# Mamba stage: the next image in twelve pieces between C's spreads, and two lists of waits in another order

## What is computed

```python
def _mamba(x, W_in, conv_w, conv_b, W_x, W_dt, b_dt, A_log, D_skip, W_out):
    ...
    u = silu(causal_conv4(xi) + conv_b)
    x_dbl = u @ W_x.T
    dt = softplus(x_dbl[..., :dt_rank] @ W_dt.T + b_dt)
    Bs, Cs = ...                       # 16 states each, per pixel
    A = -exp(A_log)
    def step(h, inp):                  # along the 3136 pixels
        dA = exp(dt_t[..., None] * A)
        h = dA * h + (dt_t * u_t)[..., None] * B_t[:, None, :]
        return (h, einsum('bdn,bn->bd', h, C_t))
    ...
    return y * silu(z) @ W_out.T

x = x + _L0(_gn(x)); x = x + _L1(_gn(x)); x = x + _L2(_gn(x))
x = x + _L3(_gn(x))      # _L3: m(x1) + x1*s1 + m(x2) + x2*s2, layer norms, projection
```

## Time and profile before

| | us |
|---|---|
| time, median of 3 runs (lowest, highest) | 6452.99 (6450.01, 6456.59) |
| the profiled execution, its own time | 6451.64 |
| its span in the trace | 6449.8 |
| busy: PE / DVE / ACT / POOL | 4509.5 / 5081.2 / 2524.9 / 4686.1 |
| Mamba stage, from 3215 us | about half of the span |

### The profile page before, as it was taken

The page is one execution under the profiler, slowest core; times in us unless marked ns, Lnnn a source line. Parts: engine busy times, 40 slices in busy tenths (PEclk is TensorE's granted clock), DMA queues, the critical chain, the costliest instruction groups (busy, mean ns, idle before and its releaser), DMA issues. The chain is left out here.

```text
span 6449.8 us, 55394 instructions
## 1 busy us (share of the span) xinstructions
PE 4509.5 (70%) x15006; PEld 2441.9 (38%) x15006; DVE 5081.2 (79%) x4078; ACT 2524.9 (39%) x3885; POOL 4686.1 (73%) x3364
## 2 busy tenths in 40 slices
PE   4888656565564756553257888888788887887887
PEld 2666523332323333232123433433344343443433
DVE  4888726776766677666558989989899898998998
ACT  1112111111111111110056666666666666666664
POOL 1666617777777777777457878878788787887887
PEclk8777766566565665655589999999999999999999
DMA  5556723434435344343235444444444544444443
GB/s 156 116 120 128 146 73 104 123 115 143 122 104 153 104 122 121 119 124 105 87 113 150 151 144 149 152 144 150 143 155 142 153 151 146 149 138 154 154 152 117
DMA packets 377439, 853.16 MB, mean 132 GB/s; under 512 B 194828, under 2 KB 237732, under 8 KB 372784
## 3 DMA queue, kind: packets, MB, share of 16 engines
q1 hardware_dynamic: 292432, 618.03, 32.7%
q0 software_dynamic: 84672, 231.32, 11.9%
HBM read 766.91 MB, written 56.48 MB: 128 GB/s over the span
## 5 line engine op out<-in xcount | busy, mean ns | idle before, releaser
L2035 POOL TENSOR_TENSOR ma_hc<-ma_h,ma_cc 128x784 f32<-128x784 f32 x1024 | 1885.1, 1848 | 628.5 <-DVE ma_h L1937 496.4
L827 POOL DMA_INDIRECT fl_quad<-table,fl_idx x1764 | 1698.5, 963 | 694.4 <-issue 537.0
L1592 PE MATMUL ma_bank<-ma_hc,ident 128*128 128x392 f32 x4096 | 1529.9, 495 | 74.5 <-POOL ma_hc L2035 74.5
L1937 DVE TENSOR_TENSOR_SCAN ma_h<-ma_da,ma_state,ma_bank 128x784 f32<-128x784 f32 x768 | 1417.4, 1846 | 168.6 <-POOL ma_hc L2035 67.0
L1810 ACT ACTIVATE ma_da<-ma_dt,ma_a_neg 128x784 f32<-128x784 f32 x1024 | 948.1, 943 | 496.1 <-DVE ma_h L1937 479.3
L978 DVE TENSOR_TENSOR fl_part<-fl_quad,fl_bank 128x2304 f32<-128x2304 f32 x196 | 500.3, 2552 | 709.6 <-DMA fl_quad<-table,fl_idx 697.0
L1925 DVE TENSOR_TENSOR ma_bank<-ma_dtu,ma_bank 128x784 f32<-128x784 f32 x1024 | 980.7, 958 | 32.7 <-PE ma_bank L1579 32.2
L1592 PEld LDWEIGHTS ma_bank<-ma_hc,ident 128*128 128x128 f32 x4096 | 709.0, 190 | 504.1 <-POOL ma_hc L2035 79.0
L1119 PE MATMUL fl_bank<-ident,fl_tap 128*128 128x128 f32 (+1 forms) x980 | 242.8, 410 | 935.8 <-DVE xres L996 875.0
L1579 PE MATMUL ma_bank<-ma_bc,ma_sel 96*128 96x512 bf16 (+1 forms) x2048 | 517.0, 334 | 451.4 <-DVE ma_h L1937 439.9
L986 DVE TENSOR_REDUCE fl_tap<-fl_part 128x576 f32<-128x2304 f32 x196 | 796.6, 4064 | 0.1
(11 more groups left out here) (220 smaller groups left out, 6095.8 us busy)
## 6 DMA issues: line engine op xcount, KB each, us to landing
ma_cc<-c_rows SPq DMA_DIRECT2D x512, 784.0 KB, 4.2
mx_win<-flat SPq DMA_DIRECT2D x64, 878.0 KB, 10.2
fl_quad<-table,fl_idx POOLq DMA_INDIRECT x1764, 2.7
table<-fl_xt SPq DMA_DIRECT2D x64, 392.0 KB
mx_mask<-in_c_mask SPq DMA_DIRECT2D x56, 294.0 KB, 4.4
ma_xs<-ma_x SPq DMA_DIRECT2D x64, 196.8 KB, 5.2
ma_xs<-ma_x SPq DMA_DIRECT2D x64, 196.5 KB, 5.7
mx_xf<-flat SPq DMA_DIRECT2D x8, 816.0 KB, 15.5
```

Source lines behind the costliest of these rows:

```text
L827: gp.indirect_dma_start(quad[i][:, kk, :], None, table, bass.IndirectOffsetOnAxis(ap=idx[i][:, kk:kk + 1], axis=0))\
L1592: ins = pe.matmul(ps_y[:, t, :], ident[:], hc[:, n % RH, at], start=False, stop=(n == DS - 1))
L1937: dve.tensor_tensor_scan(h[:, i % RH, :], da[:, i % RH, :], ps_bu[i % 2], before, ALU.mult, ALU.add).then_inc(scand, 1)
L2035: gp.tensor_tensor(hc[:, i % RH, :], h[:, i % RH, :], cc[:, i % (NGRP * GRP), :], ALU.mult)\
```

## The change

**The image in pieces.** `image` is replaced by `piece(x, n)` for n = 0 to 11: pieces 0 to 7 are the eight transfers of the shuffled half as before (8 partitions each), pieces 8 to 11 are the ordered half in four transfers of 16 partitions. The same 1568 KB go to the same places; x_in now counts 12 x 16. In the period q = 1 the pieces stand one behind a spread each: pieces 0 to 2 behind the next group's spreads 1 to 3 in group 0 (the wait for `centred` stands ahead of piece 0), 3 to 6 behind spreads 4 to 7 of group 1, 7 to 10 behind the next group's spreads 0 to 3, and 11 behind those. The first image, ahead of the loop, is loaded by the same 12 transfers in a row.

**The order of waits.** In `times_b`, `scan` (DVE) and `times_c` (POOL) the same waits are written in another order: the semaphore of the work that ends last is named last. No instruction of arithmetic is changed, and PE's and ACT's instructions stand as before.

```diff
@@ -1298,7 +1298,7 @@
     AHEAD = 3
     NGRP, GRP = 4, 2
     BR = 2 * DS
-    XIN = 9 * 16
+    XIN = 12 * 16
     with ExitStack() as ctx:
         s = Space(nc, ctx, "ma")
         xa = s.sb("xa", [P, PIX])
@@ -1408,12 +1408,14 @@
             for half, name in ((lower, "m_s1"), (upper, "m_s2")):
                 sp.dma_start(vec[half, 7:8], k[name].partition_broadcast(CH)).then_inc(consts, 16)
 
-            def image(x):
-                sp.dma_start(xa[lower, :], x).then_inc(x_in, 16)
-
-                for j in range(8):
-                    sp.dma_start(xa[CH + 8 * j:CH + 8 * j + 8, :],
-                                 x.rearrange("(g j) n -> j g n", j=8)[j]).then_inc(x_in, 16)
+            def piece(x, n):
+
+                if n < 8:
+                    sp.dma_start(xa[CH + 8 * n:CH + 8 * n + 8, :],
+                                 x.rearrange("(g j) n -> j g n", j=8)[n]).then_inc(x_in, 16)
+                else:
+                    own = slice(16 * (n - 8), 16 * (n - 8) + 16)
+                    sp.dma_start(xa[own, :], x[own]).then_inc(x_in, 16)
 
             def halves(dram, b, q):
 
@@ -1461,26 +1463,37 @@
 
             def period(b, q, post=True, norm=True, prep=True):
                 Q = NQ * b + q
+                more = q == 1 and not (isinstance(b, int) and b == NB - 1)
+                if more:
+                    later = k["x3"][bass.ds(b + 1, 1)].rearrange("b c n -> (b c) n")
                 for g in range(2):
                     G = 2 * Q + g
                     for j in range(NGRP, DS // GRP):
                         spread_c(G, g, j)
                         if j == NGRP and g == 0 and post:
                             load_residual(b, q - 1)
-                        if j == NGRP + 1 and g == 0 and q == 1 and not (isinstance(b, int) and b == NB - 1):
-                            sp.wait_ge(centred, START + NQ * b + NQ)
-                            image(k["x3"][bass.ds(b + 1, 1)].rearrange("b c n -> (b c) n"))
+                        if g == 1 and more:
+                            piece(later, j - 1)
                     if g == 0 or prep:
                         put_c(G + 1, 1 - g)
                         for j in range(NGRP):
                             spread_c(G + 1, 1 - g, j)
+                            if g == 0 and j == 1 and more:
+                                sp.wait_ge(centred, START + NQ * b + NQ)
+                            if g == 0 and j >= 1 and more:
+                                piece(later, j - 1)
+                            if g == 1 and more:
+                                piece(later, NGRP + 3 + j)
+                        if g == 1 and more:
+                            piece(later, 11)
                     if g == 1:
                         if norm:
                             stack(b, q + 2)
                         if post:
                             store(b, q - 1)
 
-            image(k["x3"][0])
+            for n in range(12):
+                piece(k["x3"][0], n)
             stack(0, 0)
             stack(0, 1)
             put_c(0, 0)
@@ -1919,19 +1932,20 @@
 
             def times_b(G, g, i):
                 V = DS * G + i
-                dve.wait_ge(bready, START + V + 1)
                 if i == 0:
                     dve.wait_ge(dtud, START + G + 1)
+                dve.wait_ge(bready, START + V + 1)
                 dve.tensor_tensor(ps_bu[i % 2], dtu[g][:], ps_bu[i % 2], ALU.mult).then_inc(bud, 1)
 
             def scan(G, m, g, i):
 
                 V = DS * G + i
+                if not (isinstance(V, int) and V < RH):
+                    dve.wait_ge(saved, START + (DS // 2) * G + (i - RH) // 2 + 1)
+                    dve.wait_ge(hcd, START + V - RH + 1)
                 dve.wait_ge(expd, START + V + 1)
+
                 dve.wait_ge(bud, START + V + 1)
-                if not (isinstance(V, int) and V < RH):
-                    dve.wait_ge(hcd, START + V - RH + 1)
-                    dve.wait_ge(saved, START + (DS // 2) * G + (i - RH) // 2 + 1)
 
                 before = zcol[:] if m == 0 else state[:, g, i:i + 1]
                 dve.tensor_tensor_scan(h[:, i % RH, :], da[:, i % RH, :], ps_bu[i % 2], before,
@@ -2025,13 +2039,14 @@
             def times_c(G, i, after_low=None):
                 V = DS * G + i
                 j = i // GRP
-                gp.wait_ge(scand, START + V + 1)
                 if after_low is not None:
                     gp.wait_ge(lowd, START + after_low)
                 if i % GRP == 0:
                     gp.wait_ge(cin[j % NGRP], START + 32 * G + 16 * (j // NGRP) + 16)
                 if not (isinstance(V, int) and V < RH):
                     gp.wait_ge(yd, START + V - RH + 1)
+
+                gp.wait_ge(scand, START + V + 1)
                 gp.tensor_tensor(hc[:, i % RH, :], h[:, i % RH, :], cc[:, i % (NGRP * GRP), :], ALU.mult)\
                   .then_inc(hcd, 1)
 
```

## The result

| | before | after | forecast |
|---|---|---|---|
| median of the runs, us | 6452.05 (6450.01 to 6456.59) | 6364.4 (6361.5 to 6366.82) | 6306 (6298 to 6332) |
| profiled execution, us | 6451.64 | 6361.5, span 6359.6 | 6305.6 |
| ratio to before | 1 | 0.9863, interval 0.9846 to 0.988 | 0.977 |

The change is a gain of 88 us where 146 were forecast. The time is that of rival A, 6366, and the question is whether A's reason is right too. All the gain lies in the Mamba stage; I start where the prediction started.

What follows compares the result with a forecast made beforehand. DVE was taken to bound the Mamba stage. From the profiled 6451.64 us, 87 for the image and 59 for the order of waits gave 6305.6, so 6306 us for the median, range 6298 to 6332.

Steps and rivals of the forecast that it cites:

- rival A: DVE's order of waits brings nothing, since the number of instructions stays and sets the gaps: 6366 us, 7%.
- What bounds the kernel: Mamba stage: DVE is the bound, busy 90.59 of 95.34 us; a change is worth what it takes from DVE's gaps.
- Part one, the image: Seven loop periods with an image load fall to their neighbours' length once the block ahead of spread 6 goes: 87.0 us.
- The prices at the dear end: Pieces in the loop: 1.5 us delay per spread; 2 us more at the last piece would cost 14 us; 0 taken.
- On small transfers: Skill's fixed 2 us per transfer: three more per image cost 6 us, 42 in all if on the path, else nothing.
- 0, within half a us: First image, ahead of the loop: the same bytes in another cut change the time by 0, within half a us.
- Part two, the order of waits: DVE in the loop: the register instruction moves ahead of the wait for bud and is covered by the multiply: 59 us.
- the steps from multiply to scan are 1.04 or 1.05 throughout: Sign in DVE's timeline that the order of waits worked: the 1.13 us steps are gone.
- a bound from below: Order of waits priced by the written-out period without register instructions: 95.34 - 93.33 = 2.01 us, 56 us over 28 periods.
- the written-out period has the same PE work at the shorter step and still runs at 93.33: Argument that PE, in whose queue B's rows stand, can follow a faster DVE, so the 59 us hold.
- B: Rival: pieces still delay ACT's xa read or spreads, 3 to 6 us per image: 6327 to 6348 us, 6%.
- C: Rival: slower than before, as spreads behind pieces land so late that POOL stands at each: 6516 us, 2%.

Runs made afterwards that it cites:

- e5: Changed kernel with DVE's waits for saved and hcd moved ahead of the multiply, expd on an instruction behind it, bud on the scan itself: 6279.0 us.
- e1: Changed kernel with the old order of waits on DVE and POOL, so only the image in pieces is left: 6370.08 us.
- e9: Kernel before with the image's nine transfers still in a row, but behind the next group's spread 3 instead of ahead of spread 6: 6366.07 us.
- e2: Kernel before with the new order of waits alone, the image still in nine transfers in a row: 6441.75 us.
- e4: Changed kernel with the scan's waits written saved, bud, expd, hcd, making bud the second wait of the instruction ahead at most steps: 6324.04 us.
- e6: Changed kernel with PE's gate projection issued one step later, behind the spread of B's next row: 6338.03 us.
- e8: Changed kernel with three matmuls by zeros added in each group to fill PE's idle time ahead of the gate: 6420.68 us.

## Why the prediction was right in one part and wrong in the other

**What bounds the kernel: right.** What was taken out of DVE's gaps came out of the period nearly one for one. From the changed kernel to e5 each of a period's 27 gaps fell by 0.10 us, 2.7 in all; the clean period fell by 2.06 (94.31 to 92.25), and y's sums took 0.57 of the difference (16.0 us over 28 periods).

**Part one, the image: right for the seven loads in the loop.** 87.0 forecast; 88.5 by e1's windows and 86 by its time (90.5 by the windows of the changed kernel, with the order of waits in it). POOL never waits for a spread, SP never for `centred`, and ACT not for xa: ACT's read of xa, at 3512.82 before, is at

```profile
3502.97 1.04 ACT L1714 ACTIVATE ma_xa<-ma_xa,gn 128x784 f32<-128x784 f32 x1
```

and stands behind no transfer. The prices at the dear end (1.5 us for a spread, 2 us at the last piece) were not called on. On small transfers the prediction has 2 us for each from the Trainium skill ("DMA: Bandwidth & Descriptors", section "Anatomy of one DMA — SWDGE (gpsimd) path"; the section that it names has the 1 MiB). In the loop, where the transfers run beside DVE's work, no run shows this cost: twelve pieces (e1) and nine (e9) differ by 4 us over seven images, within the spread of the runs.

One small term of this part was off. The first image stands on the path, ACT waits for it, and its load in another cut was put at "0, within half a us". ACT's first read before and after:

```profile
3245.59 1.04 ACT L1701 ACTIVATE ma_xa<-ma_xa,gn 128x784 f32<-128x784 f32 x1 [9.06 <-DMA ma_xa<-x]
```

```profile
3248.89 1.04 ACT L1714 ACTIVATE ma_xa<-ma_xa,gn 128x784 f32<-128x784 f32 x1 [11.22 <-DMA ma_xa<-x]
```

From the first issue of the load (3228.31 and 3229.31) it is 17.3 us before and 19.6 after. The three kernels with nine transfers have 16.5 to 17.4, the eight with twelve 18.4 to 20.2: some **2 us** for three more transfers of the same bytes. The prediction's estimate from that page, 2 us for each of three, would be 6.

**Part two, the order of waits: wrong, in two steps.** 59 us were forecast, 5.7 (e1 to after) and 14 (before to e2) measured.

The first step that failed is "the steps from multiply to scan are 1.04 or 1.05 throughout". I had two kinds of gap in the trace of before, 1.13 and 1.04, and priced the new order by the better one, because only the register instruction seemed to tell them apart. But the change put together a third kind that stood nowhere in the trace, an instruction that has `bud` as its first wait, and it takes 1.09. The written-out period was given as a bound from below because it has no register instructions; it has them not in the changed kernel either, and went from 93.33 to 94.22 all the same. So more than half of the gain in the gaps was never there (of the 64 us by which e1's 853.8 exceed 756 x 1.045, 26.4 came), and steps that had been good lost 0.04 us. Clean periods take 94.31 in place of the 93.23 that the forecast comes to (95.34 - 59/28): 28 x 1.08 = **30 us**. e4 gives the forecast its due: with 1.04 and 1.05 at most steps the clean period is 93.59 and the time 6324.

The second is "the written-out period has the same PE work at the shorter step and still runs at 93.33", taken as evidence that PE can follow. Its work is the same; its clock isn't granted the same each time. In 18 groups of 32 PE fell to 1.2 GHz behind its idle time and B's row was up to 0.86 us late. Beyond the clean length the loop's periods hold 24.6 us in the changed kernel (21 x (95.30 - 94.31) + 7 x (94.85 - 94.31)), against 5.3 (21 x (95.59 - 95.34)) that the forecast carried over: **19 us**. The 17 stalls of the loop are 14.5 us on DVE and, at 1.07 us of a period each, 18. e6 gets 17 us of the loop back by removing them (2665.2 to 2648.0).

30 and 19 are the 49 us by which the loop missed. The rest of the 56 (6361.5 against 6305.6) lies outside the loop: the two whole periods behind it took 2.9 us more than before, where 0 was said, 3.4 us lie ahead of the first scan (3294.1 before, 3297.5 after): 1.0 in the stages that the change doesn't touch, 2.3 in the load of the first image, as above. 0.2 are left.

**The rivals.** A has the time but not the reason, and its 6366 was luck: it isn't the number of instructions (e4), and that number didn't even stay the same but rose by 252 in the loop, while the gaps became less. B has its mechanism refuted in the loop: no POOL, ACT or SP wait behind a piece. C never came near. What was missing among them is the one that came: the order of waits makes one new gap for all steps, between the two old ones. It would have come out of asking which of the two waits of the instruction ahead stands first, and whether any row of the trace has that form; and if none has, the bound had to reach to no gain at all, which is rival A's 6366 and was left outside the range.

**What stays open.** Why the same idle time of 1.23 us on PE is followed by a low clock in 18 groups and not in 14, and why the kernel before, with a longer one, had it in 5 only: removing or filling the idle time stops it, but what chooses the groups wasn't found. Nor was it found why a wait instruction with `bud` first is recorded only from the signal on.

## What to carry to other kernels

Where a short operation waits for the one just ahead on its own engine, put that wait on the operation itself and let every other wait stand ahead of the earlier operation; here this was worth 85 us in 6364 for no change in the work, while "wait for it last" in the source was worth 6 to 14 us. Read from the instructions what the build makes of the written order, and if the trace has no row of that very form, let the range reach to no gain. When DVE's gaps are shortened, look at once at the engine that feeds it, at its idle times and at the clock behind them; and when a transfer holds something up, move it, and above all the wait in front of it, behind what is due soonest before cutting it up.

## What the runs showed of the hardware

- The distance from one DVE operation to a dependent one behind it depends on where the wait stands: 0.99 us as the second operation's own wait, 1.04 to 1.05 as the second wait of an instruction between and 1.09 as its first, 1.13 to 1.24 with register instructions, for a first operation of 0.95 to 0.96 us.
- PE's granted clock fell from 1.00 to 0.50 behind an idle time of only 1.23 us, with PE busy in between, in 18 of 32 groups of the changed kernel; with the idle time removed (e6) or filled (e8) it fell in none of them.
- 1568 KB in nine transfers in a row held up the 784 KB behind them in both places, to 17.5 us (before) and 19.8 us (e9) from issue to landing. Issued 4 us ahead of the use of the 784 KB they cost the kernel 88.5 us in seven images, 19.5 us ahead next to nothing (2.2 us of POOL's waits in all, e9).
- The same 1568 KB, waited for, took 16.5 to 17.4 us from the first issue to ACT's read in nine transfers and 18.4 to 20.2 in twelve.
